# Row 0 of a gated-attention and MLP kernel: all four outer products on VectorE instead of two on VectorE and two on GpSimd

## The reference, cut to what matters

```python
q, k, v = x @ Wq, x @ Wk, x @ Wv             # x: 4 rows of the batch, 512 tokens, 128 channels
gk = log_sigmoid(x @ Wgk1 @ Wgk2 + bgk2) / 16  # 16 heads of 8 channels
def step(state, inp):                        # one token after the other
    qt, kt, vt, gt = inp
    state = state * exp(gt)[..., None] + vt[..., None] * kt[..., None, :]
    return state, einsum('bhvk,bhk->bhv', state, qt)
out = layernorm_without_mean_shift(outs) * gamma + beta   # (out - mean) / sqrt(var + 1e-5)
x = layernorm(x + (out * silu(x @ Wg)) @ Wout)
x = layernorm(x + ffn(x))                    # 128 -> 512 (silu, product) -> 512 gelu -> 512 gelu -> 128
```

## Time and profile before

| | |
|---|---|
| median of 3 executions | 186.07 us (184.8 to 186.28) |
| the profiled execution's own time | 184.29 us |
| its span, first to last instruction | 182.5 us |
| busy: TensorE matmul / VectorE / ScalarE / GpSimd | 161.6 / 148.0 / 111.6 / 113.1 us |
| mean granted TensorE clock | 0.996 of full speed |

### The profile page before, as it was taken

The page is one execution under the profiler, slowest core; times in us unless marked ns, Lnnn a source line. Parts: engine busy times, 40 slices in busy tenths (PEclk is TensorE's granted clock), DMA queues, the critical chain, the costliest instruction groups (busy, mean ns, idle before and its releaser), DMA issues.

```text
span 182.5 us, 2765 instructions
## 1 busy us (share of the span) xinstructions
PE 161.6 (89%) x802; PEld 123.2 (68%) x802; DVE 148.0 (81%) x306; ACT 111.6 (61%) x179; POOL 113.1 (62%) x96
## 2 busy tenths in 40 slices
PE   0898988999879997999999699999996998999980
PEld 0755756868657774878778477577773885887770
DVE  1499989979889997998999997989999794874062
ACT  4554889992157453478683547667635669959421
POOL 8997898879609688670677678608685320670032
PEclk9999999999999999999999999999999999999998
DMA  3999900000000000000000001000000120000102
GB/s 115 313 389 416 381 18 0 0 4 0 4 0 0 2 0 0 4 2 0 0 0 0 0 0 57 0 0 0 4 0 0 48 83 0 4 0 0 57 4 63
DMA packets 6496, 8.97 MB, mean 49 GB/s; under 512 B 562, under 2 KB 5203, under 8 KB 5971
## 3 DMA queue, kind: packets, MB, share of 16 engines
q1 hardware_dynamic: 5906, 5.93, 10.2%
q0 software_dynamic: 576, 2.88, 4.1%
HBM read 7.76 MB, written 1.05 MB: 48 GB/s over the span
## 4 chain that ended last, share of the span: by engine, by line
PE 37%; DVE 13%; ACT 4%; issue 3%; POOL 3%; POOLq 0%; DVEq 0%
PE ffn L608 6%; PE ffn L617 6%; PE att L530 4%; PE ffn L586 2%; DVE y L1083 2%; PE att L655 2%; PE ffn L674 2%; PE att L643 2%; PE att L514 2%; DVE y L1087 2%; PE ffn L667 2%; PE ffn L591 2%; PE att L515 2%; DVE o_acc L1090 1%; PE att L541 1%
## 5 line engine op out<-in xcount | busy, mean ns | idle before, releaser
L1072 DVE TENSOR_TENSOR_SCAN state<-gate,att 128x512 f32<-128x512 f32 x32 | 38.3, 1208 | 1.5 <-PE att L530 1.5
L366 POOL TENSOR_TENSOR f_lo<-full,f_hi 128x512 fp32r<-128x512 f32 x18 | 23.4, 1315 | 25.9 <-DVE full L1158 18.2
L894 ACT ACTIVATE f_hi<-ffn,vec_cols 128x512 fp32r<-128x512 f32 x24 | 16.6, 690 | 25.1 <-PE ffn L617 24.9
L325 POOL TENSOR_TENSOR u_tok<-kv_tok 128x1024 f32<-128x1024 f32 (+1 forms) x12 | 27.3, 2281 | 1.9 <-DVE o_acc L1090 1.4
L608 PE MATMUL ffn<-f_hi,h_hi 128*128 128x512 f32 x96 | 27.3, 404 | 0.0
L617 PE MATMUL ffn<-f_lo,h_hi 128*128 128x512 f32 x96 | 26.6, 399 | 0.0
L340 POOL TENSOR_TENSOR o_acc<-o_acc,y 128x512 f32<-128x512 f32 x16 | 20.7, 1296 | 7.9 <-DVE y L1083 7.7
L1083 DVE TENSOR_TENSOR y<-att,state 128x512 f32<-128x512 f32 x32 | 21.1, 670 | 0.0
L608 PEld LDWEIGHTS ffn<-f_hi,h_hi 128*128 128x128 f32 x96 | 17.6, 188 | 4.7 <-ACT f_hi L886 0.9
L617 PEld LDWEIGHTS ffn<-f_lo,h_hi 128*128 128x128 f32 x96 | 17.8, 188 | 4.1
L530 PE MATMUL att<-ident,u_tok 128*128 128x128 f32 x128 | 18.5, 275 | 1.3 <-DVE u_tok L1049 0.9
(11 more groups left out here) (176 smaller groups left out, 357.9 us busy)
## 6 DMA issues: line engine op xcount, KB each, us to landing
h_raw<-in_hT SPq DMA_DIRECT2D x2, 1024.0 KB, 12.5
h_hi<-in_hT POOLq DMA_DIRECT2D x2, 1024.0 KB, 11.9
x_tok<-in_x SPq DMA_DIRECT2D x4, 256.0 KB, 5.8
out<-out_tok SPq DMA_DIRECT2D x3, 256.0 KB, 2.3
w_raw<-in_w12T SPq DMA_DIRECT2D x1, 512.0 KB, 5.5
w_hi<-in_w12T POOLq DMA_DIRECT2D x1, 512.0 KB, 8.8
xT_raw<-in_xT SPq DMA_DIRECT2D x1, 256.0 KB, 2.7
proj_raw<-in_proj SPq DMA_DIRECT2D x2, 128.0 KB, 2.3
```

The lines of the kernel that those rows point to most:

```text
L325: nc.gpsimd.tensor_tensor(u_tok[:, j].rearrange("p k (h v) -> p k h v", v=DH), v_b.unsqueeze(1).to_broadcast([P, DH, HEADS, DH]), k_b.unsq ...
L366: nc.gpsimd.tensor_tensor(lo[:, o], full_block(layer, o), hi[:, o].bitcast(F32), ALU.subtract).then_inc(pool_rested, 1)
L894: nc.scalar.activation(hidden[layer][0][:, o], bank[:], ACT.Gelu, scale=scales[:, 1 + layer, o:o + 1]).then_inc(gelu_hi_ready, 1)
L1072: nc.vector.tensor_tensor_scan(state[:, k % 3], gate[:, b], A[2 + k % 2][:], 0.0, ALU.mult, ALU.add).then_inc(scanned, 1)
```

## The change

Row 0's two outer products of GpSimd, tiles 0 and 1, go away from its stream. VectorE makes tiles 0, 1, 2, 3 in that order where it made tiles 2 and 3. Nothing else moves. `u_ready` still counts to 4.

```diff
-        U_ON_DVE, LATER_U_ON_DVE = (2, 3), 1
+        LATER_U_ON_DVE = 1
...
             pool.dma_start(w3_hi[:], w3T).then_inc(w3_hi_loaded, 16)
-            outer_products(0, [j for j in range(TILES) if j not in U_ON_DVE])
             weight_lo(0)
             weight_lo(1)
...
-            outer_product(0, U_ON_DVE[0])
-            outer_product(0, U_ON_DVE[1])
+            for j in range(TILES):
+                outer_product(0, j)
             log_gate(0)
```

## The result

The changed kernel takes 183.9 us (median of 22, 182.71 to 185.64), the kernel before, run beside it, 184.99 us (median of 22, 184.41 to 186.5). The ratio is 0.9913, 95% interval 0.9892 to 0.9934: 0.9% faster, 1.6 us by the ratio, 1.5 us by the means of all executions and 1.1 us by the medians, where 0.93 us was forecast. (The ratios leave out executions more than 1.5% above the fastest of their kernel, here two of the changed kernel at 185.51 and 185.64 us and none of the other; where that matters I give the times themselves.) The profiled execution has a span of 181.9 us against 182.5, but the span ends with the wait for the last store. The last computing instruction of VectorE starts at 178.57 us where it started at 179.48: 0.91 us.

The account below looks back on a forecast made before the run. The end of row 0's fourth outer product was taken to set when its scans start. 0 on GpSimd and -0.93 us on the path, from the median 186.07, gave 185.14 us; range 183.8 to 186.8.

Parts of the forecast that it names:

- Turns, and 1.08 to 1.21 us for a product of VectorE: Row 0's outer products: VectorE and GpSimd exclude each other at the shared port; VectorE's product alone takes 1.08 to 1.21 us.
- Rival A: VectorE's four products are truly slow under heavy load traffic, 1.98 us each; log_gate(0) 1.70 us later, 187.8 us; chance 0.05.
- Products over at 12.98: VectorE's four products, starting at 8.14 at 1.21 us each, end at 12.98 us, 1.45 us sooner than before.
- `log_gate(0)` at 13.43, 0.93 us sooner: On VectorE it waits for ScalarE's Ln and starts at about 13.43 us instead of 14.36.
- The cover of 0.45 us: VectorE's idle time between the last product and log_gate(0); products could cost 1.32 us each with the gain whole.
- GpSimd's slack of 0.31 us: End of the prologue: 0.24 of GpSimd's 0.55 us wait is eaten, 0.31 left, so its last sum comes 0.93 sooner.
- "Hidden either way": TensorE's transposes of u, even at the slow 0.26 us each, end at 15.15, before the scan wanting them at 16.3.
- "its quick rate comes later than it did, after the shorter pause": TensorE, one way to lose the 0.93 us gain before the pipeline: 185.1 to 186.1, set at 186.0; chance 0.20.
- the median's 1.78 us above it: Whole kernel: median 186.07 lies 1.78 us above the profiled execution; the same difference was kept for the forecast.
- "About 1% from no change": Measurement of the whole kernel: it tells about 1% from no change, so the 0.5% forecast counted as "within 1%".
- Rival D: Later rows' port turns fall better, or loads land sooner with GpSimd idle: another 1 us, 184.1 us; chance 0.05.

Follow-up runs that it names:

- three: Changed kernel, but GpSimd keeps one product (tile 0) and VectorE makes tiles 1, 2, 3: 184.09 us, ratio 0.9914 to the kernel before.
- turns: Changed kernel, with GpSimd also making two products of its own into a free buffer: 191.03 us, ratio 1.0321 to the kernel before.
- five: Changed kernel with one more product on VectorE ahead of the four, into a free buffer: 184.14 us, ratio 0.9942 to the kernel before.
- x2_early: Changed kernel with transpose_x(2) moved up to right behind transpose_x(1) on TensorE: 183.75 us, ratio 0.9899 to the kernel before.
- before_again: The kernel before, run once more without an edit: 186.0 us, ratio 1.0003 to the same kernel's other executions.
- filled: The kernel before with four idle transposes added on TensorE ahead of the transposes of u: 187.1 us.
- after_again: The changed kernel, run once more without an edit: 183.77 us, ratio 0.9886 to the kernel before.
- write_only: Changed kernel, with GpSimd filling four free buffers with zeros during VectorE's products: 183.86 us, ratio 0.9898 to the kernel before.
- filled_twice: The kernel before with two groups of four idle transposes on TensorE, the second behind another wait: 184.91 us, ratio 0.9978.
- pause: Changed kernel with one wait added on TensorE before the transposes of u: 184.55 us, ratio 0.994 to the kernel before.
- six: Changed kernel with two more products on VectorE ahead of the four, into free buffers: 186.52 us, ratio 1.0054 to the kernel before.
- pool_all: All four outer products on GpSimd, none on VectorE: 189.03 us, ratio 1.0166 to the kernel before.

## Why the prediction was right and wrong

- **Turns, and 1.08 to 1.21 us for a product of VectorE**: right. 1.22 us measured, 1.14 back to back; three and turns close to within 0.2 us with the same two prices, turns with the weight rest counted among the turns. Rival A (slow by load traffic) fell: the four products run under the same loads, 386 GB/s where it was 380.
- **Products over at 12.98**: 12.71, as I had left the overlap of 0.1 us each aside. It changed nothing, as the Ln was the later one.
- **`log_gate(0)` at 13.43, 0.93 us sooner**: 13.42. The cover of 0.45 us was 0.71; five used it.
- **GpSimd's slack of 0.31 us**: 0.40; passed on whole in this trace. In the execution profiled for x2_early, which gained more, this was the place where part of it was lost.
- **"Hidden either way"** for the transposes, and with it the 0 us for TensorE: this step failed. For the changed kernel the sentence holds as far as it goes: slow transposes end at 15.13 (15.15 was worked out) and the first scan isn't late. What it left out is that TensorE can stay slow far beyond the transposes, and that this happens behind the pause, so in the kernel before. I had assumed one fixed moment at which TensorE turns fast, and mentioned "its quick rate comes later than it did, after the shorter pause" only as a way to lose the gain. The runs show the opposite sign. With the pause TensorE is late in the greater part of the executions of the kernel before (77 of 120 are high; the one profiled for before_again took 185.45 us against 184.29), and the change, by closing the pause, takes that away (2 of 28). The one profiled execution of before, at 184.29 us, was one without this cost, and I took the median's 1.78 us above it as a constant to be carried over.
- So the forecast of 0.93 us is the gain of an undisturbed execution, and the missing term is worth 0.2 us by the medians and 0.7 us by the ratio in the first comparison, about 1.1 us in the later ones (185.78 - 183.77 - 0.93). That 0.93 us lies so near the 1.1 us of the first medians is partly luck: the kernel before was high in only 10 of its 22 executions there, in 67 of 98 later.
- **"About 1% from no change"** was wrong too. The interval of the measurement is 0.2% to either side, so even the 0.5% of the forecast would have been told from no change, without the missing term.
- **The time itself**: 185.14 us forecast, 183.9 measured. Of the 1.24 us between them 1.08 are the kernel before, whose median fell from 186.07 in three executions to 184.99 in 22, and 0.16 are gain. The predicted range (183.8 to 186.8) held the median by 0.1 us, again by luck. Rival D's 184.1 is nearer, but its mechanism didn't come: the loads land as before (`weight_lo(0)` at 14.60 against 14.68).

## What to carry to other kernels

Here GpSimd was no help to VectorE for products with two SBUF inputs: four took 6.29 us split two and two, 5.43 split one and three, and 4.63 on VectorE alone. Before splitting such work, count both engines' work in one line. When a change closes or opens a pause of TensorE, look at the pace of its matmuls behind the pause, in more than one execution; here a pause of 0.92 us could cost 1.4 us more. And where the profiled execution is well below the median, ask what the others have that it hasn't, before the difference is carried over as a constant.

## What was not expected of the hardware

TensorE turned from 0.43 to 0.23 us for 512 columns at very different moments, with the same matmuls in the same order ahead of it up to 8.6 us at least: between 8.6 and 9.6 us in the traces of x2_early, turns and filled, between 13.3 and 14.8 us in those of before, changed, after_again, write_only, three, five and filled_twice, at 18.2 to 18.4 us in those of before_again, pause and six, and at 25.4 us in pool_all. The late ones are all behind a pause of 0.92 us or more, but not every such pause makes it late: in the first trace of before TensorE became fast within it. The Trainium skill, "TensorE: Matmul & The Clock Gate", section "Part 1: The HAM clock gate (the "warmup" mystery)", says that this moment isn't tied to the kernel's start and varies between runs by 0.5 us to either side. These traces agree that it varies, but by far more: 8.7 and 13.3 us behind the same work. What the pause does to it is seen in two forms: the turn to fast comes late (before_again: a pause of 0.92 us, slow until 18.4 us, the granted clock shown as 1.00 throughout), or the clock falls afterwards (filled: a pause of 2.34 us, then 0.50 for some 7 us). In the first form the granted clock of the profile shows nothing, and only the starts of the matmuls do.
